# Layer 0 attention: scores in two fp32r terms from stacked heads, row sums by DMA instead of turns, evictions over pairs of banks

## The reference

```python
B, T, C = x.shape          # 2, 512, 256
H = 16; hd = C // H        # 16
scale = 1.0 / math.sqrt(hd)
q, k, v = (proj(Wq), proj(Wk), proj(Wv))
scores = jnp.einsum('bhqd,bhkd->bhqk', q, k) * scale
w = jnp.where(causal, jax.nn.relu(scores - ATTN_THRESHOLD), 0.0)   # ATTN_THRESHOLD = -0.1
w = w / (jnp.sum(w, axis=-1, keepdims=True) + EPS)                 # EPS = 1e-6
out = jnp.einsum('bhqk,bhkd->bhqd', w, v)
return jnp.einsum('btc,oc->bto', out.swapaxes(1, 2).reshape(B, T, C), Wo)
```

## Time and profile before

| | |
|---|---|
| median of 3 runs | 520.43 us (520.12 to 520.55) |
| the profiled execution, its own time | 520.81 us |
| its span, first to last instruction | 519.1 us |
| busy: PE, PEld, DVE, ACT, POOL | 475.5, 399.3, 384.5, 335.8, 240.5 us |
| granted TensorE clock, mean | 0.983 of full |
| instructions | 10798 |

### The profile page before, as it was taken

The page is one execution under the profiler, slowest core; times in us unless marked ns, Lnnn a source line. Parts: engine busy times, 40 slices in busy tenths (PEclk is TensorE's granted clock), DMA queues, the critical chain, the costliest instruction groups (busy, mean ns, idle before and its releaser), DMA issues.

```text
span 519.1 us, 10798 instructions
## 1 busy us (share of the span) xinstructions
PE 475.5 (92%) x3848; PEld 399.3 (77%) x3848; DVE 384.5 (74%) x675; ACT 335.8 (65%) x940; POOL 240.5 (46%) x167
## 2 busy tenths in 40 slices
PE   2799997999999977999999999998998699999995
PEld 1454653688888976799999999987997688889884
DVE  4455597778563689899899989999998975553534
ACT  3555564725534357998898988877988799333230
POOL 0377536321432477457656655656358821320001
PEclk9999997999999988999999999999999999999998
DMA  8500010023321000000000000001001312100101
GB/s 272 180 15 3 3 42 0 1 91 78 115 73 42 1 1 1 3 20 21 23 20 23 23 5 18 23 20 42 3 21 42 87 38 63 42 0 1 35 7 42
DMA packets 8612, 19.97 MB, mean 38 GB/s; under 512 B 1392, under 2 KB 2928, under 8 KB 8432
## 3 DMA queue, kind: packets, MB, share of 16 engines
q1 hardware_dynamic: 8560, 19.29, 11.8%
HBM read 18.23 MB, written 1.05 MB: 37 GB/s over the span
## 4 chain that ended last, share of the span: by engine, by line
PE 77%; DVE 11%; ACT 5%; issue 4%; DMA 1%; POOL 0%; DVEq 0%; POOLq 0%; SPq 0%; ACTq 0%
PE psum L499 17%; PE psum L501 16%; PE psum L500 15%; PE psum L553 5%; PE psum L725 4%; PE psum L715 4%; PE psum L737 4%; PE psum L571 4%; PE psum L696 3%; ACT probs L977 3%; DVE minus_max L1253 2%; PE psum L705 2%; DVE roped L1238 1%; DVE square_sums L1215 1%; DMA raw_chunks<-in_w 1%
## 5 line engine op out<-in xcount | busy, mean ns | idle before, releaser
L977 ACT ACTIVATE probs<-psum,minus_max 128x128 f32<-128x128 f32 x256 | 92.0, 399 | 16.0 <-issue 8.1
L1372 POOL TENSOR_TENSOR rope_sin_part<-qkv_rows,sin_weighted 128x640 f32<-128x640 f32 x32 | 51.2, 1623 | 48.6 <-DVE rope_cos_part L1222 42.3
L1381 POOL TENSOR_TENSOR rms_inverse<-rms_inverse,minus_half 128x20 f32<-128x20 f32 x16 | 63.5, 3970 | 1.3
L977 ACT ACTIVATION_READ_ACCUMULATOR probs<-psum,minus_max 128x1 f32 x256 | 60.7, 237 | 0.0
L945 ACT CAST hidden_high<-hidden 128x512 fp32r<-128x512 f32 x32 | 19.9, 622 | 61.1 <-DVE hidden L1168 61.1
L1253 DVE TENSOR_REDUCE minus_max<-psum 128x4 f32<-128x512 f32 x64 | 42.0, 685 | 14.6 <-PE psum L715 13.6
L499 PE MATMUL psum<-x_t_high,ug_high_low 128*128 128x512 f32 x128 | 51.1, 399 | 0.0
L501 PE MATMUL psum<-x_t_high,ug_high_low 128*128 128x512 f32 x128 | 50.7, 396 | 0.0
L500 PE MATMUL psum<-x_t_low,ug_high_low 128*128 128x512 f32 x128 | 50.5, 395 | 0.0
L499 PE MATMUL psum<-qkv_high_low,x_t_high 128*128 128x384 f32 x128 | 47.1, 368 | 3.1 <-ACT qkv_rows L950 1.7
L1247 DVE TENSOR_TENSOR probs<-probs,prob_inverse 128x512 f32<-128x512 f32 x64 | 48.0, 750 | 2.2
(11 more groups left out here) (145 smaller groups left out, 1381.4 us busy)
## 6 DMA issues: line engine op xcount, KB each, us to landing
raw_chunks<-in_ug SPq DMA_DIRECT2D x8, 512.0 KB, 3.9
raw_chunks<-in_wout SPq DMA_DIRECT2D x16, 256.0 KB, 2.8
raw_chunks<-in_qkv SPq DMA_DIRECT2D x8, 384.0 KB, 3.2
raw_chunks<-in_x SPq DMA_DIRECT2D x2, 512.0 KB, 4.6
...
```

The lines of the kernel that those rows point to most:

```text
L977: e = nc.scalar.activation(pr[:, c, q, :], o[:, q * P:(q + 1) * P], ACT.Exp, bias=negm[:, c, q:q + 1], accum_out=psum1[:, c, q:q + 1])
L1372: last = nc.gpsimd.tensor_tensor(ov[:, :, :, z, :], rv[:, :, :, 1 - z, :], sv[:, :, :, z, :], ALU.mult)
L1381: nc.gpsimd.tensor_tensor(r, r, half[:], ALU.pow).then_inc(rr_done, 1)
```

## The change

**Scores.** q and k are now split into high and low parts in fp32r. Wq, Wk and the input side of Wo have their features reordered on the host, so that even and odd heads alternate from row to row (row parity). ACT writes the high parts (`qk_rows`), DVE the low parts. DMAs from SBUF to SBUF (`beside`, `beside_odd`) then lay out 32 rows for each head: its 16 features twice, on even and odd rows, with k's high and low parts on both, and q's high part on the even and its low part on the odd rows. DVE copies the whole, 3 x 512 columns, into `qk_stack` (`stack0`), once for the even and once for the odd heads. `scores0` makes two fp32r matmuls for each key block and head where one fp32 matmul stood: k high with (q high, q low), then k low with the same.

**Sums.** `v_and_ones` has 33 columns a head: a one beside each value. `pv0` now gives, on even and odd rows, a value sum and the row sum. No turns are needed: ACT copies the bank out with the epsilon as a bias on the rows of the sums, DMAs bring the sums to the rows of their values (`move_sums`, `move_odd`), DVE takes the reciprocal of 128 x 512 sums and multiplies (`divide0`, for half of the heads of a batch), ACT rounds (`high0`), DVE subtracts (`low0`). `turn0` and `at0` are gone.

**Evictions.** The four heads of a part lie in two pairs of neighbouring banks. ACT evicts one pair in one instruction, DVE the other. A pair has semaphores of its own and comes free as a whole.

**Order.** All four tables are new, and SP's issues up to load 8 stand in a table, SYNC_FIRST. In layer 0 `ln` is cut into halves. The order of two places on DVE and one on SP is shown below the diff.

```diff
@@ scores on PE
-                heads = [claim(("scores0", b, hg, part, h4)) for h4 in range(HG)]
+                    pe.wait_ge(s0_done[odd], KB * b + m + 1)
+                heads = []
+                for pr in range(2):
+                    bank, done = claim_pair(("scores0", b, hg, part, pr))
+                    heads += [(ps[:, bank + h2, :], done) for h2 in range(2)]
...
-                        mm = nc.tensor.matmul(heads[h4][0][:, at:at + w], k0[r, m, odd, keys], q0[r, m, kb * P:T],
-                                              start=True, stop=True)
+                    for z in range(2):
+                        for h4 in range(HG):
+                            r = slice(32 * h4, 32 * h4 + 32)
+                            mm = nc.tensor.matmul(heads[h4][0][:, at:at + w], s0[r, m, odd, z, keys],
+                                                  s0[r, m, odd, 2, kb * P:T], start=z == 0, stop=z == 1)
@@ DMAs on SP
+            def beside(b, z, m):
+                emptied(sp, ("qk0", b, z, m))
+                at = slice(0, 2) if z else slice(2, 3)
+                src = r0[m][0::2, 1, at].bitcast(F32)
+                sp.dma_start(r0[m][0::2, 0, at].bitcast(F32), src).then_inc(heads_in[0][m], 16)
+                src = src if z else qlow[m][0::2, :]
+                dst = r0[m][1::2, 0, at].bitcast(F32)
+                sp.dma_start(dst if z else dst.rearrange("p a t -> p (a t)"), src).then_inc(heads_in[0][m], 16)
...
+            def move_odd(b, m):
+                emptied(sp, ("pv0", b, 2 * m + 1))
+                sp.dma_start(sums0[b][1::2, m, :], odd_out[0::2, :]).then_inc(odd_in[m], 16)
+                sp.wait_ge(sums_in[m], 16 * (b + 1))
+                sp.dma_start(parts0[b][1::2, m, :], odd_out[1::2, :]).then_inc(odd_in[m], 16)
@@ evictions
-                for h4 in (0, 2):
-                    o, done = take(act, ("scores0", b, hg, part, h4))
+                o, done = take_pair(act, ("scores0", b, hg, part, 0))
+                nc.scalar.activation(wt[:, hg % 2, 0:2, at:at + w], o[:, :, 0:w], ACT.Relu,
+                                     bias=bias0[:]).then_inc(done, 1)
...
-                for h4 in (1, 3):
+                o, done = take_pair(dve, ("scores0", b, hg, part, 1))
+                nc.vector.tensor_scalar(wt[:, hg % 2, 2:4, at:at + w], o[:, :, 0:w], -ATTN_THRESHOLD, 0.0,
+                                        ALU.add, ALU.max).then_inc(done, 1)
@@ DVE
-                nc.vector.tensor_scalar(k0[:, m, 1, :], o, parity[:, 1:2], None, ALU.mult).then_inc(done, 1)
+                nc.vector.tensor_tensor(r0[m][:, 1, 1].bitcast(F32), o, r0[m][:, 1, 0].bitcast(F32),
+                                        ALU.subtract).then_inc(done, 1)
...
+                nc.vector.scalar_tensor_tensor(out=qlow[m][:], in0=o, scalar=float(HD0) ** -0.5,
+                                               in1=r0[m][:, 1, 2].bitcast(F32), op0=ALU.mult,
+                                               op1=ALU.subtract).then_inc(done, 1)
+            def stack0(b, m, odd):
+                dve.wait_ge(heads_in[odd][m], (32 if odd else 64) * (b + 1))
+                if b:
+                    pair_filled(dve, ("scores0", b - 1, 2 * m + odd, 2, 1))
+                nc.vector.tensor_copy(s0[:, m, odd], r0[m][:, odd].bitcast(F32)).then_inc(s0_done[odd], 1)
-            def turn0(b, hg):
-                o, done = take(dve, ("turn0", b, hg))
-                link(nc.vector.tensor_scalar(rs0[:], ov[:, :, :, HD0], ATTN_EPS, None, ALU.add))
-                link(nc.vector.reciprocal(ri0[:], rs0[:]))
+            def divide0(b, m):
+                dve.wait_ge(sums_in[m], 16 * (b + 1))
+                emptied(dve, ("pv0", b, 2 * m))
+                dve.wait_ge(odd_in[m], 32 * (b + 1))
+                sums = sums0[b][:, m, :]
+                link(nc.vector.reciprocal(sums, sums))
+                nc.vector.tensor_tensor(sums, parts0[b][:, m, :], sums, ALU.mult).then_inc(divided, 1)
+            def low0(b, m):
+                dve.wait_ge(out0_high, KB * b + m + 1)
+                nc.vector.tensor_tensor(atl[:, m, :], sums0[b][:, m, :], ath[:, m, :].bitcast(F32),
+                                        ALU.subtract).then_inc(out0_low, 1)
@@ PE, before wo0
-                emptied(pe, *[("at0", b, kb) for kb in range(KB)])
+                pe.wait_ge(out0_low, KB * (b + 1))
```

More of the change, by code:

```diff
@@ L79 @@
 CHUNK_NO = {(name, c): k for k, (name, c, _, _) in enumerate(CHUNKS)}
+PREP_FIRST = next(ch[:2] for ch in CHUNKS if ch[2] in ("pair", "tree"))
 CHUNK_COLS = {"x": 1024, "w0": 1024, "had": P, "down0": 1024, "ug0": 1024, "msk": 1024, "eye": P,
@@ L141 @@
+SYNC_LOADS = 1 + max(step[1] for step in SYNC_FIRST if step[0] == "load")
 TENSOR_FILL = [("up", 0, 10), ("down", 0, 8), ("down", 0, 9), ("up", 0, 11), ("xt", 2, 0), ("down", 0, 10),
@@ L336, in post_ln_two_layers @@
         with ExitStack() as s:
-            place(s, "below_tree", [4096], F32)
-            tree = place(s, "down_tree", [2, NI, C], F32)
+            r0, qlow = [None] * KB, [None] * KB
+            for m in range(KB):
+                r0[m] = place(s, f"qk0_rows{m}", [2, 3, T], F32R)
+                qlow[m] = place(s, f"q0_low{m}", [T], F32)
+                if m == 0:
+                    place(s, "until_tree", [512])
+                    tree = place(s, "down_tree", [2, NI, C], F32)
         with ExitStack() as s:
@@ L414, in post_ln_two_layers @@
         emptied_ = [sem(f"bank{i}_emptied") for i in range(8)]
+        pair_full = [sem(f"banks{2 * i}{2 * i + 1}_full") for i in range(RING // 2)]
+        pair_emptied = [sem(f"banks{2 * i}{2 * i + 1}_emptied") for i in range(RING // 2)]
         ch_in = [sem(f"chunk_in{i}") for i in range(SLOTS)]
@@ new lines, in move_odd @@
+            def move_odd(b, m):
[3 more added lines that the diff above has]
+                sp.dma_start(parts0[b][1::2, m, :], odd_out[1::2, :]).then_inc(odd_in[m], 16)
+            do = dict(load=load_chunk, const=const, tree=tree_load, rows=rows, tables=tables, beside=beside, beside_odd=beside_odd, move_sums=move_sums, move_odd=move_odd)
@@ L844, in _ @@
+            for step, *args in SYNC_FIRST:
+                do[step](*args)
+            for n in range(SYNC_LOADS, len(LOADS)):
                 load_chunk(n)
@@ L874, in chunk @@
                     src = tree[:, 1, 4 * c:4 * c + 4, :].rearrange("p a b -> p (a b)")
+                if (name, c) == PREP_FIRST:
+                    act.wait_ge(out0_low, KB)
+                    for odd in range(2):
+                        act.wait_ge(s0_done[odd], KB * B)
                 if (name, c) in FFN1_CHUNKS:
@@ L906, in pv0, with high0 @@
                     return
+                m, odd = divmod(hg, 2)
                 o, done = take(act, ("pv0", b, hg))
-                n = b * NHG + hg
-                if n:
-                    filled(act, ("turn0",) + divmod(n - 1, NHG))
-                nc.scalar.copy(osb[:], o).then_inc(done, 1)
-            def at0(b):
-                for kb in range(KB):
-                    high(("at0", b, kb), ath[:, kb, :])
+                if not (b or m):
+                    act.wait_ge(const_in["row_consts"], 16)
+                if odd:
+                    if b or m:
+                        act.wait_ge(odd_in[1 - m], 32 * (b + m))
+                    nc.scalar.activation(odd_out[:], o, ACT.Identity, bias=row_consts[:, 1:2]).then_inc(done, 1)
+                else:
+                    if b:
+                        filled(act, ("qk0", b, 0, KB - 1))
+                    nc.scalar.activation(parts0[b][:, m, :], o, ACT.Identity, bias=row_consts[:, 0:1]).then_inc(done, 1)
+            def high0(b, m):
+                act.wait_ge(divided, KB * b + m + 1)
+                if b:
+                    filled(act, ("y", 0, b - 1, 1))
+                nc.scalar.copy(ath[:, m, :], sums0[b][:, m, :]).then_inc(out0_high, 1)
             def xt(layer, b):
@@ L1334, in scores0 @@
             def scores0(b, hg, part):
-                emptied(pool, *[("scores0", b, hg, part, h4) for h4 in range(HG)])
+                for pr in range(2):
+                    pair_, n = job["scores0", b, hg, part, pr]
+                    pool.wait_ge(pair_emptied[pair_], n + 1)
                 for kb in PART_BLOCKS[part]:
```

204 lines of the change are left out of this document (116 added, 88 removed), and 74 rows, old and new, of tables (GPSIMD_FIRST, SCALAR_FIRST, TENSOR_FIRST, VECTOR_FIRST).

## The result

The changed kernel takes 535.59 us (four executions, 534.16 to 536.94) against 520.49 for the kernel before, measured beside it: a ratio of 1.029, 95% interval 1.0256 to 1.0324. "Slower" was the forecast, but at 526.0, and 535.6 lies outside the range of 514.5 to 534: 15 us lost where 5.5 were expected. In what follows, executions more than 1.5% above the fastest of their kernel are left out of the ratios (three of four in e3_tree_later, which leaves it without a ratio, and two of eight in e6_both).

The account below looks back on a forecast made before the run. PE bounds the stage now; with DVE at 90.4 us against PE's 84 the bound moves to DVE. Walked handovers end the stage at 124 against 118.6, +5.5: 526.3 from 520.8, less 0.4 for the median, 526.0; range 514.5 to 534.

Parts of the forecast that it names:

- VectorE's sum: DVE's work in the stage up to batch 1's turned normed rows: +19.7 us, to 90.4 us.
- TensorE's sum: PE's work in the same stage: 99.9 - 16 = 84 us, with scores 9 less and turns 6.8 less.
- that rival: Score matmuls: fp32r row groups do not overlap, 4.8 us a group where 1.9 was taken; 538 us, chance 0.05.
- The waits behind the divisions: PE idle behind the four divide0: 2.8 us, 3.5 at wo0(0), 5.5 up to up 0, 5 before wo0(1).
- The start: First handover: stack0 done at 19.6, v0 covers until 17.6, PE one score part (1.1 us) behind.
- Place 2: qk0 among the scores: DVE idle about 1.7 us twice; batch 1's second-part eviction ends at 57, not 51.5.
- The step that failed: PE's clock in the stage: 3.4 us lost now, about as much behind gaps of 5 us, nothing added.
- The turning point of the reciprocal: The divisions: a wide reciprocal below about 2.3 us decides for the faster rival; 3.7 was taken.
- The cheap reciprocal: The divisions: at 0.68 us each the four waits shrink by 3 us, 12 in all; 514 us, chance 0.16.
- The signs of being wrong: Trace checks: reciprocal below 2.3 us; 32 pairs in over 2.5 us; stage over before 118.

Follow-up runs that it names:

- e3_tree_later: Changed kernel with three of POOL's tree steps moved to later places; 537.6 us, no ratio.
- e6_both: Changed kernel with each division replaced by a copy of the sums onto themselves, plus the added matmuls of e5; 524.8 us.
- e5: Changed kernel plus matmuls on PE whose result nobody reads, ahead of its waits, placed so that they can't come late; 527.85 us.
- e1: Changed kernel with each wide reciprocal replaced by a copy of the sums onto themselves; 519.05 us.
- c8: Changed kernel with the edit of e9, plus added matmuls that nobody reads ahead of six of its waits; 527.4 us.
- c3: Changed kernel with divisions moved and done in halves, plus 18 added matmuls in the first 30 us; 535.2 us, 533.1 without these matmuls.
- c7: Changed kernel with later steps moved, nine score parts evicted by ACT alone, added matmuls and later tree steps; 535.6 us, 529.15 without the last two.
- e9: Changed kernel with ACT evicting all four heads at five score parts around the divisions, which stay in place; 529.1 us.

## Why the prediction was wrong

- **VectorE's sum** held: 90.4 forecast, 92.7 measured. Reciprocals 13.4 for 14.8; the stacking copies 10.8 for 7.7, since some ran beside POOL (the median one took 1.0). The row of the narrow reciprocal gave 7.0 ns a column, the wide ones 6.25 ((3.344 - 1.743) us over 256). The 8.3 estimated from the Trainium skill (VectorE: DVE Perf Modes, "First, the fixed hardware budget") lies above both, as I had put it.
- **TensorE's sum** held at full clock: fp32r score matmuls of four heads run side by side, 0.74 + 0.62 + 0.68 = 2.04 us a group for 1.9 forecast, and that rival is out. In e5 PE is busy 99.2 us up to the stage's end, 13.1 of them with added matmuls: 86.1 for 84.
- **The waits behind the divisions** held: 2.60, 2.79, 3.68 and 4.20 us for 2.8, 3.5, 5.5 and 5. All four were put rather too long. The start held nearly (first score matmul at 20.33 for 19.6). Place 2 held only at full clock: the eviction put at 57 ended at 62.9, and at 58.3 in e5.
- **The step that failed** is "The clock loses 3.4 us now and would lose about as much behind gaps of 5 us: nothing added". It lost 17.0. Waits of 2 to 4 us could bring half clock for three to seven microseconds (in windows of one microsecond), and there were seven such stretches, not one. Two lie between 21 and 36, behind the late stacking and the evictions after it, and lost 5.1 us of clock. Those from 59, 76, 103 and 124 lie at the waits behind the four divisions and lost 10.2. The one from 97 lies behind a wait of 2.35 ahead of the last scores and lost 1.7; it is the old one of the earlier trace rows, 3.22 us at 85 and 0.51 behind it. So the row was at hand: I walked four new waits of that size and did not multiply. Four more times 3.4 us on top of 526.0 would have allowed up to 539.6, and a range over 535.6. That 3.4 + 4 x 3.4 is just the measured 17.0 is luck: the four lost 2.6 each, and the start, where the walk had nothing, the rest.
- **The turning point of the reciprocal** was wrong too. I had "below about 2.3 us" from a sum of the four waits; at 2.0 to 2.2 with the copy the kernel is still 1.46% slower than before.
- **The cheap reciprocal** as a rival said 514. 519.05 was measured, with three of ten executions at 515; e1 still loses 5.1 us of clock.
- **The signs of being wrong** that I had named (a reciprocal below 2.3 us, 32 pairs in over 2.5, the stage over before 118) all stayed away, at 3.34, 2.04 and 136.4. None of them looked at the clock.

What is shown: without the wide reciprocal all of the loss is gone; four of them cost the kernel before 11.6 us; matmuls that keep the clock at full give the changed kernel back 7.7 of the 15 (11.8 between the two profiled executions), and PE's time over the forecast is busy time, not idle time. What stays open: why e5 and c8, with their clock at the level of the kernel before or better, spread over 525 to 532; why c3 and c7 gained nothing by the first 18 of these matmuls; and how much of e9's gain is DVE's time and how much the clock behind it (clock lost 13.6 for 17.0).
